# Gate weights of an expert layer broadcast by a DMA from DRAM instead of by matmuls

## The reference

```python
cur = x
for r in range(R):
    flat = cur.reshape(-1, h)
    logits = flat @ Wg[r] + bg[r]
    vals, idx = jax.lax.top_k(logits, TOPK)
    w = jax.nn.softmax(vals, axis=-1)
    cw = jnp.sum(jax.nn.one_hot(idx, E, dtype=flat.dtype) * w[..., None], axis=1)
    hmid = jax.nn.gelu(jnp.einsum('nh,ehf->enf', flat, W1) + b1[:, None, :])
    y = jnp.einsum('enf,efh->enh', hmid, W2) + b2[:, None, :]
    out = jnp.einsum('ne,enh->nh', cw, y)
    cur = cur + out.reshape(b, s, h)
```

## Time and profile before

| | |
|---|---|
| time before, median of 3 (lowest, highest) | 528.86 us (527.92, 533.05) |
| time of the profiled execution | 533.33 us |
| its span | 531.6 us |
| PE busy | 463.6 us (87%), 2692 matmuls |
| DVE busy | 351.8 us (66%) |
| ACT busy | 324.8 us (61%) |
| POOL busy | 133.0 us (25%) |
| mean granted TensorE clock | 0.931 |

### The profile page before, as it was taken

One profiled execution on the slowest core, in us unless ns is written; L12 is line 12 of the kernel. 1 busy time (PEld: TensorE's weight loads), 2 busy tenths in 40 slices (PEclk: granted clock), 3 DMA queues, 4 the chain that ended last, 5 costly groups with the idle time before them and its releaser, 6 DMA issues.

```text
span 531.6 us, 8533 instructions
## 1 busy us (share of the span) xinstructions
PE 463.6 (87%) x2692; PEld 356.8 (67%) x2692; DVE 351.8 (66%) x967; ACT 324.8 (61%) x632; POOL 133.0 (25%) x195
## 2 busy tenths in 40 slices
PE   3777999988993998579999867999999999999995
PEld 2446777755831686448777745878778787878783
DVE  4375677767589565546778845858585767777653
ACT  2444767642255442035665527898988989898892
POOL 7060000212165100114545420121112221111121
PEclk9976999998998898857999977999999999999999
DMA  8911111000300000001111000000000000000001
GB/s 296 368 25 31 31 32 28 19 1 1 159 1 0 1 1 1 0 21 40 32 31 28 14 0 1 1 2 0 1 0 0 0 0 0 0 0 1 2 0 39
DMA packets 12754, 16.07 MB, mean 30 GB/s; under 512 B 4008, under 2 KB 11304, under 8 KB 12080
## 3 DMA queue, kind: packets, MB, share of 16 engines
q1 hardware_dynamic: 12288, 14.79, 8.8%
q10 hardware_dynamic: 432, 0.85, 0.4%
HBM read 10.92 MB, written 0.52 MB: 22 GB/s over the span
## 4 chain that ended last, share of the span: by engine, by line
PE 64%; DVE 15%; issue 9%; ACT 6%; POOL 3%; DMA 2%; SPq 1%; ACTq 0%; POOLq 0%; DVEq 0%
PE ps L1229 6%; PE ps L1274 4%; PE ps L1544 4%; PE ps L1545 4%; PE ps L1543 4%; PE ps L1562 4%; PE ps L1561 4%; PE ps L1560 4%; PE ps L1241 3%; POOL xnT L447 2%; DVE masked L816 2%; PE ps L1551 2%; PE ps L1462 2%; PE ps L1149 2%; DVE big L933 1%
## 5 line engine op out<-in xcount | busy, mean ns | idle before, releaser
L1078 DVE TENSOR_TENSOR bigr<-ps,bigr 128x512 fp32r<-128x512 f32 x128 | 86.3, 689 | 57.8 <-ACT ps L681 57.8
L541 ACT ACTIVATE big<-ps 128x512 f32<-128x512 f32 (+1 forms) x128 | 68.7, 548 | 52.9 <-PE ps L1241 50.9
L680 ACT ACTIVATE bigr<-ps,b 128x512 fp32r<-128x512 f32 x128 | 89.8, 702 | 3.6 <-PE ps L1545 0.7
L681 ACT ACTIVATE ps<-ps,b 128x512 f32<-128x512 f32 x128 | 86.6, 677 | 0.0
L447 POOL TENSOR_TENSOR xnT<-xnT,big 128x512 f32<-128x512 f32 x32 | 41.4, 1293 | 162.4 <-DVE big L1085 162.4
L1229 PE MATMUL ps<-bigr,qk 128*128 128x256 f32 (+1 forms) x224 | 53.8, 323 | 5.4 <-DMA bigr<-qk 2.8
L823 DVE TENSOR_REDUCE nmax<-ps 128x2 f32<-128x512 f32 x64 | 42.6, 688 | 18.8 <-PE ps L1229 18.4
L1241 PE MATMUL ps<-qk,bigr 128*128 128x256 f32 (+1 forms) x256 | 51.2, 284 | 1.0 <-ACT big L541 0.7
L1543 PE MATMUL ps<-k1hi,w1hi 128*128 128x512 f32 x128 | 51.5, 402 | 0.0
L1544 PE MATMUL ps<-k1hi,w1lo 128*128 128x512 f32 x128 | 51.3, 401 | 0.0
L1545 PE MATMUL ps<-k1lo,w1hi 128*128 128x512 f32 x128 | 51.2, 400 | 0.0
(11 more groups left out here) (200 smaller groups left out, 864.3 us busy)
## 6 DMA issues: line engine op xcount, KB each, us to landing
bigr<-qk SPq DMA_DIRECT2D x128, 32.0 KB, 1.9
wi<-in_wi SPq DMA_DIRECT2D x1, 2048.0 KB, 7.6
wo<-in_wo SPq DMA_DIRECT2D x1, 2048.0 KB, 12.1
big<-in_sel SPq DMA_DIRECT2D x1, 1024.0 KB, 8.6
wo<-in_w SPq DMA_DIRECT2D x1, 1024.0 KB, 4.8
wi<-in_w SPq DMA_DIRECT2D x1, 1024.0 KB, 6.9
x<-in_x SPq DMA_DIRECT2D x1, 512.0 KB, 5.5
ctxT<-in_ctxT ACTq DMA_DIRECT2D x1, 512.0 KB, 4.9
```

Of the source, the lines that this page charges most:

```text
L541: act.activation(prob[:, h % 8, c], ps[:, 2 + h % 2, c], ACT.Exp, scale=DH ** -0.5).then_inc(s(L + "_exp"), 1)
L680: act.activation(ghi[:, u % 2, c, :], ps[:, c, :], ACT.Gelu_apprx_tanh, bias=b1[:, u % E1, c:c + 1])
L681: act.activation(ps[:, c, :], ps[:, c, :], ACT.Gelu_apprx_tanh, bias=b1[:, u % E1, c:c + 1]).then_inc(s("ff1_gel"), 1)
L1078: v.tensor_tensor(glo[:, u % 2, c, :], ps[:, c, :], ghi[:, u % 2, c, :].bitcast(f32), ALU.subtract).then_inc(s("ff1_glo"), 1)
```

## The change

The gate rows no longer pass through a matmul and a copy per unit. ACT's copy of the transposed rows (now 4 partitions, plain float32, no high and low part) is written by SP to a DRAM scratch `gates`, and once that has landed a second DMA reads it into all 128 partitions of the half's four `cwb` tiles (each partition gets 4 x 512 floats, 1 MB in all). `combine` waits for that DMA once a half. `spread`, `spread_weights`, the selection matrix with its load, its two memsets on POOL and its conversion on DVE go; so do three of the four instructions of `gate_b`.

```diff
-        cwT = sb("cwT", [P, 2, HALF], f32r)
-        sel_er = sb("sel_er", [P, E1, P], f32r)
+        cwT = sb("cwT", [E1, 2, HALF])
...
-        cwr = sb("cwr", [P, NT * E0], f32r)
-        cwhl = sb("cwhl", [P, 4, 2 * E1])
-        sel_e = sb("sel_e", [2 * E1, E1, P])
+        gates = nc.dram_tensor("gates", (2, E1, HALF), f32, kind="Internal").ap()
...
-            load("ff1", sel_e[:, :, :], w["sel_e"])
...
             padded_keys("xa1")
+            for Hf in range(2 * R1):
+                hf = Hf % 2
+                sp.wait_ge(s("ff1_ctev"), 1 + Hf + 1)
+                sp.dma_start(gates[hf], cwT[:, hf, :]).then_inc(s("ff1_gates"), 16)
+                sp.wait_ge(s("ff1_gates"), 16 * (Hf + 1))
+                sp.dma_start(cwb[:, E1 * hf:E1 * hf + E1, :], gates[hf].partition_broadcast(P)
+                             ).then_inc(s("ff1_cwb%d" % hf), 16)
...
-            pool.memset(cwT[:, :, :].bitcast(f32), 0.0).then_inc(s("ff1_zero"), 1)
-            pool.memset(sel_er[:, :, :].bitcast(f32), 0.0).then_inc(s("ff1_zero"), 1)
...
-            def spread_weights(U, u):
-                act.wait_ge(s("ff1_bcd"), U + 1)
-                act.activation(cwb[:, u % 8, :], ps[:, 6, :], ACT.Copy).then_inc(s("ff1_cwb"), 1)
...
-                act.activation(cwT[0:2 * E1, hf, :], ps[0:2 * E1, bank, :], ACT.Copy).then_inc(s("ff1_ctev"), 1)
+                act.activation(cwT[:, hf, :], ps[0:E1, bank, :], ACT.Copy).then_inc(s("ff1_ctev"), 1)
...
                     if not (last and u == 7):
-                        spread_weights(U0 + u + 1, u + 1)
                         gelus(U0 + u + 1, u + 1)
...
-                dve.wait_ge(s("ff1_zero"), 2)
-                own.mark(v.tensor_copy(sel_er[0:2 * E1, :, :], sel_e[:, :, :]))
...
-                own.step(v.scalar_tensor_tensor(cw[:, 0:m], dif[:, 0:m], 1.0, selh[:, 0:m], ALU.add, ALU.mult))
-                own.step(v.tensor_copy(cwr[:, 0:m], cw[:, 0:m]))
-                c3, r3 = (a[:, 0:m].rearrange("p (n e) -> p n e", e=E1) for a in (cw, cwr))
-                own.mark(v.tensor_copy(cwhl[:, :, 0:E1], r3.bitcast(f32)))
-                v.tensor_tensor(cwhl[:, :, E1:2 * E1], c3, r3.bitcast(f32), ALU.subtract).then_inc(s("ff1_cwd"), 1)
+                v.scalar_tensor_tensor(cw[:, 0:m], dif[:, 0:m], 1.0, selh[:, 0:m], ALU.add, ALU.mult
+                                       ).then_inc(s("ff1_cwd"), 1)
...
-            def combine(U, u):
+            def combine(U, u, r):
                 dve.wait_ge(s("ff1_dn"), 2 + U + 1)
-                dve.wait_ge(s("ff1_cwb"), 1 + U + 1)
+                if u % E1 == 0:
+                    dve.wait_ge(s("ff1_cwb%d" % (u // E1)), 16 * (r + 1))
...
-                    last = pe.transpose(ps[0:2 * E1, bank, n * P:n * P + P], cwhl[:, n, :], ident[:, :])
+                    last = pe.transpose(ps[0:E1, bank, n * P:n * P + P], cw[:, n * E1:n * E1 + E1], ident[:, :])
...
-            def spread(U, u):
-                u = u % (2 * E1)
-                pe.wait_ge(s("ff1_cwb"), U + 1)
-                pe.matmul(ps[:, 6, :], sel_er[:, u % E1, :], cwT[:, u // E1, :], start=True, stop=True
-                          ).then_inc(s("ff1_bcd"), 1)
...
                     if not (last and u == 7):
-                        spread(U0 + u + 1, u + 1)
                         up(U0 + u + 1, u + 1)
...
             pe.wait_ge(s("ff1_ctev"), 2)
-            spread(0, 0)
             pe.wait_ge(s("xa1_res"), TPB + TPB * B)
```

More of the change, by code:

```diff
@@ L459, in _ @@
             act.sem_inc(s("ff1_ctev"), 1)
-            act.sem_inc(s("ff1_cwb"), 1)
             for name, dst, src in (("ctx", ctxT[:, :], "ctxT"), ("ctx", wctx[:, :, :], "wctx"),
@@ L708, in _ @@
             gelus(0, 0)
-            act.wait_ge(s("ff1_zero"), 2)
             gate_rows(0, 0, 6)
             evacuate_xnT("ff1", 1, 5)
-            spread_weights(0, 0)
             with act.Fori(0, R1 - 1) as r:
@@ L1032, in constants @@
             def constants():
-                dve.wait_ge(s("ld_ff1"), 6 * 16)
-                dve.wait_ge(s("ff1_zero"), 2)
-                own.mark(v.tensor_copy(sel_er[0:2 * E1, :, :], sel_e[:, :, :]))
+                dve.wait_ge(s("ld_ff1"), 5 * 16)
                 own.mark(v.tensor_scalar(maskf[:, :], mask_i[:, :], 0, None, ALU.not_equal))
@@ L1110, in round_ @@
                         add_experts(0)
-                    combine(U0 + u, u)
+                    combine(U0 + u, u, r)
                     if u == 0:
@@ L1121, in _ @@
             dve.wait_ge(s("ln_xnT"), ln("ff1", 2) + 2)
-            per = 2 * 1 + 2 * (9 + 3)
+            per = 2 * 1 + 2 * 9
             with dve.Fori(0, R1 - 1) as r:
@@ L1517, in gate_rows @@
                 for n in range(4):
-                    last = pe.transpose(ps[0:2 * E1, bank, n * P:n * P + P], cwhl[:, n, :], ident[:, :])
+                    last = pe.transpose(ps[0:E1, bank, n * P:n * P + P], cw[:, n * E1:n * E1 + E1], ident[:, :])
                 last.then_inc(s("ff1_ct"), 1)
             def first_logits():
-                pe.wait_ge(s("ld_ff1"), 6 * 16)
+                pe.wait_ge(s("ld_ff1"), 5 * 16)
                 pe.wait_ge(s("ln_xnT"), ln("ff1", 2) + 1)
@@ L1644, in shape_constants @@
         c[n] = (np.arange(E)[None, :] < np.arange(E)[:, None]).astype(f)
-    c["sel_e"] = np.ascontiguousarray(np.broadcast_to(
-        (np.arange(2 * E1)[:, None] % E1 == np.arange(E1)[None, :])[:, :, None], (2 * E1, E1, P))).astype(f)
     return c
```

## The result

The changed kernel takes 520.96 us (median of 4 runs, 520.27 to 526.80); the kernel before, with one more run beside it, 528.39 (527.92 to 533.05). The ratio is 0.986, with a 95% interval of 0.9815 to 0.9904: faster by 1.4%, 7.4 us. The prediction was 520.9.

A forecast was written before the change was run, and what follows sets the result against it. PE's number of matmuls was taken to bound the last stage, with DMA free. Savings of 7.05 + 0.9 = 7.95 us off the median 528.86 gave 520.9 us; the range was 518.7, less about 1 for the spread of runs, to 526.5.

The forecast's parts named there:

- `spread` goes, 7.05 us: On PE in the last stage: 30 of 32 `spread` matmuls removed at 0.235 us each save 7.05 us.
- the waiting place: PE ahead of unit 4 or 0: the wait for ACT's gate copy stays, 0.17 us, plus a slow first matmul.
- the slack of DVE's gate chain at `up(3)` and `up(7)`: DVE's `split_gelus` before these: bank 0 ready 0.18 us before PE needs it after the change.
- the rival of the gate chain: DVE's gate chain becomes the bound: 5.6 of 7.95 us given back, 526.5; chance 0.16 together with nothing gained.
- The beginning, 0.9 us: Stage start: `up(1)` starts 1.3 us sooner, some lost to PE's slow clock; between 0.7 and 1.2, taken 0.9.
- the lower bound: Stage start: clock rises at the same moment as before, about 0.6 us of the gain is lost, leaving 0.7.
- ACT and DVE count for nothing: Last stage: ACT's 32 fewer copies and DVE's three fewer `gate_b` instructions a half save nothing.
- At the start and in the cross attention, nothing: Two POOL memsets and one DVE copy removed before the stage: zero, at most twice 0.95 and 0.62 us.
- The DMA path, 7.0 us: Eight times, from ACT's copy through DRAM write and broadcast: 7.0 us in sum, bounds 6.9 and 11.1, hidden.
- The doubt: Rival on the 1 MB broadcast: engines reading the same 8 KB make it slow, beyond 10.5 us; chance 0.08.
- What hides it: Cover before `combine(4)` is 12.07 us, 5.1 to spare; at the first half, `combine(0)` leaves only 0.7 us.
- the sum: Whole kernel: 7.05 us for `spread` plus 0.9 for the stage's beginning, 7.95 us saved.

The follow-up runs named there:

- the two repeats: The changed kernel measured twice more, unchanged, as base for other experiments: ratios 0.989 and 0.9903 to the kernel before, stage 198.2 us both times.
- the last experiment: Changed kernel without PE's gate-copy wait ahead of `up(4)` and `up(0)`, three waits moved behind `up(1)`: 516.5 us, ratio 0.9762 to the kernel before.

## Why the prediction was right

The mechanism held: the matmul put back on PE returns the time, the copy put back on ACT returns nothing, and the DMA path is hidden in all eight halves. Time and sign were right. By its steps:

**`spread` goes, 7.05 us.** Too much by a little. The six middle halves shrank by 24.83 - 24.01 = 0.82 us each, not 0.94. Two steps were off, both in the last places where PE depends on its neighbours.

The first is the waiting place: I let the gate copy keep its distance to `up(3)` and left 0.27 us there. PE now loses 0.36, in six halves: 6 x 0.09 = 0.5 us. Part of the way is seen on ACT. Before, it began `gelus(3)` 0.04 us after bank 0 was complete, and its `spread_weights` had ended just ahead of that:

```profile
392.54 0.60 ACT L672 ACTIVATE big<-ps 128x512 f32<-128x512 f32 x1 [0.30 <-PE ps L1551]
```

Afterwards, here at the same place of the other half, `gelus(7)`, it starts 0.11 us after it, as the timelines of PE and ACT of the changed kernel show:

```profile
360.32 0.40 PE L1539 MATMUL ps<-k1lo,w1hi 128*128 128x512 f32 x1
```

```profile
360.83 0.69 ACT L681 ACTIVATE bigr<-ps,b 128x512 fp32r<-128x512 f32 x1 [0.82 <-PE ps L1539]
```

(360.32 + 0.40 = 360.72 to 360.83.) Everything behind it on ACT is that much later, the copy too. That this later start is what costs PE the 0.09 us is not shown, and neither is that ACT starts late because it stood idle. With the copies back on ACT it starts as late, and PE loses as much. With the matmul back on PE it starts as late too, yet the place costs 0.27 again, as that kernel's PE timeline has it (0.40 and 0.34 from start to start):

```profile
369.85 0.40 PE L1553 MATMUL ps<-bigr,w2hi 128*128 128x512 f32 x1
370.25 0.50 PE L1543 MATMUL ps<-w1lo,w1hi 128*128 128x512 f32 x1
370.59 0.40 PE L1537 MATMUL ps<-k1hi,w1hi 128*128 128x512 f32 x1
```

And in the last round ACT stands idle for 0.75 us at this place and starts 0.04 us after the bank (480.40 + 0.40 = 480.80 to 480.84, in the changed kernel):

```profile
480.40 0.40 PE L1539 MATMUL ps<-k1lo,w1hi 128*128 128x512 f32 x1
```

```profile
480.84 0.69 ACT L681 ACTIVATE bigr<-ps,b 128x512 fp32r<-128x512 f32 x1 [0.75 <-PE ps L1539]
```

So the cause of the 0.09 us stays open.

The second is the slack of DVE's gate chain at `up(3)` and `up(7)`, 0.18 us by the prediction. It is used up. In the changed kernel's PE timeline the weight load of an `up(7)` waits for `split_gelus`, and the second matmul starts 0.30 us after the first:

```profile
359.75 0.19 PEld L1537 LDWEIGHTS ps<-k1hi,w1hi 128*128 128x128 f32 x1 [0.23 <-DVE bigr L1071]
359.79 0.46 PE L1537 MATMUL ps<-k1hi,w1hi 128*128 128x512 f32 x1
360.09 0.39 PE L1538 MATMUL ps<-k1hi,w1lo 128*128 128x512 f32 x1
```

Before, the second matmul of `up(3)` started 0.23 us after the first, which stands at 392.34:

```profile
392.57 0.40 PE L1544 MATMUL ps<-k1hi,w1lo 128*128 128x512 f32 x1
```

The delay stands in five halves, some 0.06 us each, 0.3 us in all. So the rival of the gate chain was there, at a twentieth of its price. Both losses are absent in the kernel with the matmul back, which for this reason cost 6.4 us more and not 7.3. That the wait for the gate copy remains, as forecast, is shown by the kernel that took it out.

**The beginning, 0.9 us.** 0.56 in place of it. The last matmul of `up(1)` starts 5.53 us after the gate copy's start now (326.33 against 320.80), and before it was 6.09 (332.68 against 326.59); in the two repeats it is 5.62, which makes 0.47. Both are below the 0.7 to 1.2 of the prediction. PE's wait ended later than I took it, and the clock worked as the lower bound had it. These are PE's first rows, then windows (columns as in rows 1):

```profile
322.21 0.79 PE L1537 MATMUL ps<-k1hi,w1hi 128*128 128x512 f32 x1 [2.90 <-ACT xnT L472]
322.80 0.63 PE L1538 MATMUL ps<-k1hi,w1lo 128*128 128x512 f32 x1
```

```profile
322.40:325.00 2.60, 2.60 (x7) 2.02 (x8) 0.00 (x0) 1.02 (x2) 0.00 (x0) 0.50 0.47 195
```

ACT's evacuation ends at 321.85, the matmul starts 0.36 later and is slow; then eight matmuls instead of six run at 0.50 of the clock, that is 1.2 GHz. In the last experiment PE has no such pause, and its granted clock is 1.00 there.

The three losses, 0.5, 0.3 and 0.9 - 0.56 = 0.34, make up about the 1.1 us by which the stage fell short of 7.95.

**ACT and DVE count for nothing.** Right for ACT by the copy put back. DVE's three instructions that went had no experiment of their own; the matmul put back leaves 0.4 us for them and all else.

**At the start and in the cross attention, nothing.** Right as far as the runs can tell.

**The DMA path, 7.0 us.** It took 6.2: 0.02 for SP to start, 1.41 from the issue of the write to that of the broadcast (I had 2.1), and 4.8 as forecast. The doubt was whether 128 reads of the same 8 KB are slow. They aren't, by the median of 4.8 us: in the same profile the loads of 1 MB with separate rows landed after 4.7 and 6.8 us, the first alone, the second behind it. The rule on rows at large powers of two in the Trainium skill, "DMA: Bandwidth & Descriptors", section "Latency and other measured facts", did not carry over to this: 4.8 us measured against the 12.5 estimated from it. Half of this case's own rate, 2.3 + 2 x 2.48 = 7.3 us by the prediction's numbers, is ruled out by the median too.

**What hides it.** Right in size for the cover: with two broadcasts `combine(0)` waited 2.41 us where 2.7 had been expected of the time, and of the later halves only the one with a slow broadcast waited; with three all eight waited. The 0.18 us of slack that the cover was reckoned with were not there, as above. The first half is the one place with little room: with one broadcast the gate weights come 2.5 us early, with two they are late.

The forecast against the median hit closer than its sum: the sum was 1.1 us too large, and the median's gain of 7.4 us lies between the stage's 6.8 and the sum, well inside the interval. That the forecast of 520.9 met the median of 520.96 so closely is luck: the medians of the same kernel in the two repeats are 523.59 and 524.82.

## What to carry to other kernels

In a stretch where one engine never stops, count its slots first: here a matmul that only spreads data over partitions cost its slot, and the copy that followed it on an idle engine cost nothing. Then look at the places where that engine nearly waits for another: a shorter stretch eats their slack, and here 0.18 us that had been reckoned as spare were gone. A transfer through DRAM can replace both if its whole path, issue to landing twice over, is shorter than the distance from its source to its first reader, and its first use, where the pipeline is still filling, has to be checked by itself. When a step goes, look again at the waits around it: PE's wait for the gate copy, which `spread` had needed, was worth 2.5 us, and moving the waits ahead of `up(1)`, of which the one for ACT's evacuation of the tokens ended last, another 2.5, against the 6.8 us of the change.

## What the runs showed of the hardware

- A broadcast of 1 MB from 8 KB of DRAM into 128 partitions landed after 4.8 us (median of eight, 4.3 to 6.1), no slower than 1 MB of separate rows (4.7). In nearly every profile one or two broadcasts took 6 us or more, 7.6 at the most; one of these made the unexpected wait of the doubled broadcast. What makes them slow stays open.
- The round trip of an 8 KB write from SBUF to DRAM, from its issue to that of a DMA that waits for it, was 1.39 to 1.44 us, less than the 1.9 us of a 32 KB copy inside SBUF and the 2.3 us of a store of 256 KB.
- ACT started 0.04 us after the (modelled) end of the matmul that it waited for in some places and 0.11 in others, and the idle time ahead of it (0.10 to 1.00 us) doesn't tell which: after 0.75 us of idling it was 0.04 in the last round.
- In the kernel with three broadcasts PE's granted clock fell to 0.50 at pauses of 6.6, 2.8, 2.9 and 2.5 us and stayed at 1.00 at others of 2.6 and 3.1 us; a middle half in which it fell took some 1.5 us more.
- 1 MB transfers beside PE, ACT and DVE left no mark on PE: its starts stay 0.23 us apart with a mean of 42 GB/s of traffic in the window, and five halves kept their length with twice the broadcasts.
